# Groups of 128 rows in a streamed adjacency product: 21 blocks of 384 columns in place of 16 of 504

## What is computed

```python
# x: [8192, 64], adj: [8192, 8192], u: [8192, 64], all float32
keep = (u >= 0.1)
x_drop = x * keep / 0.9
y = x + adj @ x_drop
out = (y - mean(y)) / sqrt(var(y) + 1e-5)      # over the 64 columns of each row
```

## Time and profile before

| | |
|---|---|
| three runs, median | 643.01 us (642.99 to 643.07) |
| the profiled execution, its own time | 643.25 us |
| its span, first to last instruction | 641.5 us |
| TensorE busy with matmuls | 514.2 us, 80% |
| VectorE, ScalarE, GpSimd busy | 8%, 2%, 3% |
| moved by DMA | 274.80 MB, 428 GB/s over the span |
| TensorE's granted clock, mean | 0.93 of full |

### The profile page before, as it was taken

How to read it: one execution, slowest core, us unless ns; L and a number is a source line. 1 busy time by engine, 2 the same in 40 slices (tenths; PEclk the granted TensorE clock), 3 DMA queues, 4 the chain that set the end, 5 groups by cost and what they waited for, 6 DMA issues and landing times.

```text
span 641.5 us, 5637 instructions
## 1 busy us (share of the span) xinstructions
PE 514.2 (80%) x2308; PEld 175.9 (27%) x2308; DVE 48.6 (8%) x230; ACT 10.8 (2%) x18; POOL 18.0 (3%) x27
## 2 busy tenths in 40 slices
PE   0397888778988797797788779788797788689796
PEld 0132223222222232232232223222232232223225
DVE  2100101010010100101010010100001010000102
ACT  0000000000000000000000000000000000000000
POOL 0000000000000000000000000000000000000000
PEclk9998888998979798898989989798898989989999
DMA  9999999999999999999999999999999999999998
GB/s 374 423 448 436 429 432 440 416 440 425 430 436 450 412 449 440 429 426 443 413 440 429 430 432 454 426 432 443 423 430 439 420 437 447 428 416 428 434 422 335
DMA packets 9962, 274.80 MB, mean 428 GB/s; under 512 B 1388, under 2 KB 1642, under 8 KB 2666
## 3 DMA queue, kind: packets, MB, share of 16 engines
q1 hardware_dynamic: 9660, 274.60, 99.5%
q10 hardware_dynamic: 300, 0.16, 0.1%
HBM read 272.66 MB, written 2.10 MB: 428 GB/s over the span
## 4 chain that ended last, share of the span: by engine, by line
DMA 70%; PE 27%; issue 1%; SPq 0%; DVE 0%; POOL 0%; POOLq 0%; ACT 0%; DVEq 0%
DMA raw<-adj_dram 70%; PE acc L173 26%; SPq L132 0%; PE turned L193 0%; POOL rstd L268 0%; DVE stats L238 0%; POOLq L47 0%; ACT sums L211 0%; DVE rows L234 0%; SPq L137 0%; SPq L135 0%; SPq L136 0%; DVE moments L243 0%; POOLq L273 0%; DVE final_normed L261 0%
## 5 line engine op out<-in xcount | busy, mean ns | idle before, releaser
L173 PE MATMUL acc<-raw,dropped 128*64 128x504 f32 x2048 | 488.5, 637 | 93.3 <-POOLq L273 89.3
L173 PEld LDWEIGHTS acc<-raw,dropped 128*64 128x64 f32 x2048 | 152.9, 147 | 417.2 <-issue 291.5
L234 DVE TENSOR_TENSOR rows<-turned,x_sb 126x256 f32<-126x256 f32 x16 | 6.8, 425 | 541.8 <-PE turned L193 541.8
L268 POOL TENSOR_TENSOR rstd<-var_eps,minus_half 126x4 f32<-126x4 f32 x16 | 16.2, 1013 | 613.4 <-DMA raw<-adj_dram 330.2
L193 PE MATMUL turned<-join,sums 128*126 128x64 f32 x128 | 17.5, 279 | 10.9 <-ACT sums L211 10.9
L193 PEld LDWEIGHTS turned<-join,sums 128*126 128x126 f32 x128 | 15.3, 189 | 24.8 <-ACT sums L211 24.8
L211 ACT COPY sums<-acc 128x504 f32<-128x504 f32 x16 | 9.3, 579 | 616.3 <-PE acc L173 616.3
L249 DVE TENSOR_SCALAR normed<-rows,moments,rstd 126x64 f32 x64 | 15.7, 310 | 29.4 <-POOL rstd L268 29.4
L183 PE MATMUL final_turned<-x_final,eye 128*128 128x64 f32 x2 | 0.7, 449 | 18.1 <-DVE dropped L229 18.1
L238 DVE BATCH_NORM_STATS2 stats<-rows 126x6 f32<-126x64 f32 x64 | 9.7, 214 | 0.5
L173 PE MATMUL final_acc<-raw,dropped 128*64 128x128 f32 x128 | 7.3, 274 | 0.0
(11 more groups left out here) (14 smaller groups left out, 2.6 us busy)
## 6 DMA issues: line engine op xcount, KB each, us to landing
raw<-adj_dram SPq DMA_DIRECT2D x30, 5544.0 KB, 26.8
raw<-adj_dram SPq DMA_DIRECT2D x14, 5040.0 KB, 29.0
raw<-adj_dram SPq DMA_DIRECT2D x2, 3024.0 KB, 21.9
raw<-adj_dram SPq DMA_DIRECT2D x2, 2520.0 KB, 27.5
raw<-adj_dram SPq DMA_DIRECT2D x2, 2016.0 KB, 23.6
raw<-adj_dram SPq DMA_DIRECT2D x2, 1512.0 KB, 26.9
dropped<-u_dram SPq DMA_DIRECT2D x1, 2048.0 KB, 7.8
x_sb<-x_dram SPq DMA_DIRECT2D x1, 2048.0 KB, 12.3
```

The costliest lines, as they stand in the source:

```text
L173: last = nc.tensor.matmul(sum_bank[t * D:(t + 1) * D, 0:width], dropped[:, t * PAIRS + q, :], raw[:, s, start:start + width], start=(q == ...
L234: nc.vector.tensor_tensor(rows[:, :, :], turned[0:ROWS, 0:GROUPS, :], x_sb[0:ROWS, bass.ds(b * GROUPS, GROUPS), :], ALU.add).then_inc(turn ...
L268: nc.gpsimd.tensor_tensor(rstd[:, :], var_eps[:, :], minus_half[0:ROWS, :], ALU.pow).then_inc(rstd_ready, 1)
```

## The change

A block takes 3 groups of 128 rows, 384 columns, and there are 21 blocks; the 64th group of 128 rows is the last group. All rows of `adj` and of the output are divided as [128 partitions, 64 groups], without a remainder, and so the last group's `x` stands in `x_sb` already and its output rows lie 64 rows apart. SyncE's loop runs one block further, with whole slots, and only the last block is loaded in parts. The stores have 128 partitions in one DMA each. `PARTS`, `SLOT_PAIRS` and `FINAL` are as they were.

```diff
-ROWS = 126
-GROUPS = 4
+ROWS = P
+GROUPS = 3
-BLOCKS = CHUNKS // GROUPS
+BLOCKS = (CHUNKS - 1) // GROUPS
...
-    out_dram = out[0:ROWS * CHUNKS, :].rearrange("(p g) d -> p (g d)", p=ROWS)
+    out_dram = out.rearrange("(p g) d -> p (g d)", p=P)
...
-            sp.dma_start(x_final[:, :], x[ROWS * CHUNKS:N, :]).then_inc(x_final_loaded, DMA)
             for s in range(SLOTS):
                 load_slot(0, s)
-            with sp.Fori(1, BLOCKS - 2) as b:
+            with sp.Fori(1, BLOCKS - 1) as b:
                 for s in range(SLOTS):
                     sp.wait_ge(multiplied, (b - 1) * SLOTS + s + 1)
                     load_slot(b, s)
-            for s in range(SLOTS - 1):
-                sp.wait_ge(multiplied, (BLOCKS - 3) * SLOTS + s + 1)
-                load_slot(BLOCKS - 2, s)
-            sp.wait_ge(multiplied, (BLOCKS - 2) * SLOTS)
-            for n, (s, q0, q1) in enumerate(PARTS):
-                if s == SLOTS - 1:
-                    load_part(BLOCKS - 2, n)
...
-            for p0, p1 in [(0, EVEN), (EVEN, ROWS)]:
-                store_blocks(sp, p0, p1, 0, BLOCKS - 1)
-            sp.wait_ge(blocks_stored, 4 * DMA)
+            store_blocks(sp, 0, BLOCKS - 1)
+            sp.wait_ge(blocks_stored, 2 * DMA)
...
-            pe.wait_ge(x_final_loaded, DMA)
...
-            nc.tensor.matmul(final_turned[:, 0:D], eye[:, :], x_final[:, :], start=True, stop=False)
+            nc.tensor.matmul(final_turned[:, 0:D], eye[:, :], x_sb[:, CHUNKS - 1, :], start=True, stop=False)
...
-            for p0, p1 in [(0, EVEN), (EVEN, ROWS)]:
-                store_blocks(act, p0, p1, BLOCKS - 1, BLOCKS)
+            store_blocks(act, BLOCKS - 1, BLOCKS)
...
-            act.dma_start(out[ROWS * CHUNKS:N, :], final_normed[:, :]).then_inc(final_stored, DMA)
+            act.dma_start(out_dram[:, (CHUNKS - 1) * D:CHUNKS * D], final_normed[:, :]).then_inc(final_stored, DMA)
...
-            for s in range(1, SLOTS - 1):
+            for s in range(1, SLOTS):
                 pass_slot(BLOCKS - 2, s)
-            for n, (s, q0, q1) in enumerate(PARTS):
-                if s == SLOTS - 1:
-                    pass_part(n, 1)
-            for n, (s, q0, q1) in enumerate(PARTS):
-                pass_part(n, 2 if s == SLOTS - 1 else 1)
+            for n in range(len(PARTS)):
+                pass_part(n)
                 if n == 1:
                     rsqrt(BLOCKS - 2)
...
-    full = adj[:split].reshape(ROWS, BLOCKS, GROUPS, P, TILES, PAIRS).transpose(1, 3, 5, 4, 2, 0)
-    final = adj[split:].reshape(P, P, TILES, PAIRS).transpose(1, 3, 2, 0)
+    groups = np.asarray(adj).reshape(P, CHUNKS, P, TILES, PAIRS)
+    full = groups[:, :CHUNKS - 1].reshape(P, BLOCKS, GROUPS, P, TILES, PAIRS).transpose(1, 3, 5, 4, 2, 0)
+    final = groups[:, CHUNKS - 1].transpose(1, 3, 2, 0)
```

More of the change, by code:

```diff
@@ L29 @@
 FINAL = [(0, 8), (8, 16), (16, 22), (22, 26), (26, 29), (29, 31), (31, 32)]
-EVEN = ROWS // DMA * DMA
 P_DROP = 0.1
@@ L57, in dropout_matmul_layernorm @@
         x_sb = sbuf("x_sb", [P, CHUNKS, D])
-        x_final = sbuf("x_final", [P, D])
         dropped = sbuf("dropped", [P, CHUNKS, D])
@@ L70, in dropout_matmul_layernorm @@
         rstd = sbuf("rstd", [ROWS, GROUPS])
-        normed = sbuf("normed", [ROWS, CHUNKS, D])
+        normed = sbuf("normed", [ROWS, BLOCKS * GROUPS, D])
         final_stats = sbuf("final_stats", [P, 6])
@@ L84, in dropout_matmul_layernorm @@
         x_loaded = semaphore("x_loaded")
-        x_final_loaded = semaphore("x_final_loaded")
         u_loaded = semaphore("u_loaded")
@@ L105, in dropout_matmul_layernorm @@
         turned_free = semaphore("turned_free")
-        rows_ready = semaphore("rows_ready")
         stats_ready = semaphore("stats_ready")
@@ L116, in dropout_matmul_layernorm, with store_blocks @@
         block = ctx.enter_context(nc.Block())
-        def store_blocks(engine, p0, p1, b0, b1):
-            engine.dma_start(out_dram[p0:p1, b0 * GROUPS * D:b1 * GROUPS * D],
-                             normed[p0:p1, b0 * GROUPS:b1 * GROUPS, :]).then_inc(blocks_stored, DMA)
+        def store_blocks(engine, b0, b1):
+            engine.dma_start(out_dram[:, b0 * GROUPS * D:b1 * GROUPS * D],
+                             normed[:, b0 * GROUPS:b1 * GROUPS, :]).then_inc(blocks_stored, DMA)
         @block.sync
@@ L273, in pass_slot, with pass_part @@
                 pool.sem_inc(landed, IN_SLOT[s])
-            def pass_part(n, loads):
-                pool.wait_ge(part_loaded[n], loads * DMA)
+            def pass_part(n):
+                pool.wait_ge(part_loaded[n], DMA)
                 pool.sem_inc(landed, 1)
@@ L316 @@
     from concourse.bass_utils import run_bass_kernel_spmd
-    adj = np.asarray(adj)
-    split = ROWS * CHUNKS
-    full = adj[:split].reshape(ROWS, BLOCKS, GROUPS, P, TILES, PAIRS).transpose(1, 3, 5, 4, 2, 0)
-    final = adj[split:].reshape(P, P, TILES, PAIRS).transpose(1, 3, 2, 0)
+    groups = np.asarray(adj).reshape(P, CHUNKS, P, TILES, PAIRS)
+    full = groups[:, :CHUNKS - 1].reshape(P, BLOCKS, GROUPS, P, TILES, PAIRS).transpose(1, 3, 5, 4, 2, 0)
+    final = groups[:, CHUNKS - 1].transpose(1, 3, 2, 0)
     arrays = {
```

## The result

The changed kernel takes 644.47 us (median of 12 runs, 644.03 to 644.70) against 643.00 us for the kernel before (12 runs, 642.63 to 643.26). The ratio is 1.0022, 95% interval 1.0015 to 1.0030: slower by 0.22%, 1.47 us. The forecast was 643.6 us, with a range of 642.3 to 645.0. The range holds the time and the sign of the sum is right, but 0.59 us were forecast and 1.47 measured.

What follows compares the result with a forecast made beforehand. The loads were taken as the bound, in the middle and at the end. Twelve more loads (+0.73 us) and `x_final`'s load (-0.14) sum to +0.59 us, giving 643.6 us (+0.09%), range 642.3 to 645.0.

Steps and rivals of the forecast that it cites:

- Twelve more loads: Loads of `adj_dram` go from 56 to 68, at 0.061 us each: +0.73 us (0.62 to 2.2).
- likeliest case: The forecast itself, 643.6 us, with its own range of 643.4 to 643.9 us; chance 0.61.
- second fetch: Rival: another instruction fetch among the loads, from ScalarE's longer written-out code; 644.8 us, slower by 0.28%; chance 0.06.
- dearer rows: Rival: rows of the pieces cost more, 0.18 us a load, 645.1 us; point of decision 0.12 us; chance 0.08.
- signs of being wrong: Block at 29.15 us or more, 1.2 us loss at TensorE's third start missing or doubled, end chain changed over 0.5 us.
- Within 0.2%: Outcome of no difference a measurement can tell (0.2% is 1.3 us); chance 0.72, against slower 0.22 and faster 0.06.
- `x_final`'s load: Its 32 KB load leaves the queue ahead of all of `adj`: -0.14 us, bounds 0 and -0.46.
- The stores at nothing: Bulk and last-block stores as one DMA each, and last store's scattered rows, priced 0; last store's bounds -0.3 to +0.7 us.
- The fetch of instructions stays: Instruction packet still costs 1.16 us at TensorE's third start; rival that it moves out: 642.4 us, chance 0.11.
- The pitch: Rival: `adj` rows 96 KB apart instead of 126 KB slow the loop's reads, up to 686 us; chance 0.04.
- The reads get faster: Rival: every row now starts at a multiple of 512 B; with fetch gone and shorter end, some 641.5 us; chance 0.06.
- The scattered last store: Rival: last store's 256 B rows, now 16 KB apart, take over 0.7 us longer: 644.4 us; chance 0.03.

## Why the prediction was right, and where it was not

**The loads bound the kernel before and after, and TensorE, VectorE, GpSimd and ScalarE's added work is hidden.** Right. The five more copies, turnings and powers cost nothing; with the layout of `raw` put back, the block takes 29.093 us, where 29.09 was worked out from the loads alone.

**Twelve more loads, +0.73 us at 0.061 us each.** The mechanism was right, and so was the place; the size of this term is the step that went wrong. The price was that of slots 44352 B apart, and the change itself moved the slots. At 9.7 ns a row a whole load costs 8 x 9.7 = 78 ns, and that holds for all of them, not for the twelve: 60 x 0.078 = 4.7 us for the whole loads, where the prediction has 60 x 0.061 = 3.7. So the term was about +1.7 us instead of +0.73, and with -0.14 for `x_final` it gives the 1.6 to 1.7 us by which the last landing moved. The prediction goes through the change's edits of queues and instructions and nowhere asks how the slots of `raw` will lie: the line that declares `raw` is the same before and after.

**Why the range still held.** In part by luck. The loads cost 1.0 us more than the sum has, and the end came out 0.5 us shorter, which hid half of that. What was left lies outside the likeliest case's own 643.4 to 643.9 us; it lies inside the full range because that was drawn up to 645.0 for a second fetch and for dearer rows. By the prediction's signs of being wrong it is at the edge twice: the block's 29.145 us against 29.15, and the end's 0.5 us against 0.5. "Within 0.2%", which had 0.72, can't be told from "slower": the ratio is 1.0022, with 1.0015 to 1.0030.

**A price of each load.** It is one of each row. At 8 rows for a DMA engine in every load the two are the same, so nothing in the sum hung on it.

**`x_final`'s load, -0.14 us.** Nothing measures it alone. It is in the balance of the last landing, which closes within 0.1 us.

**The stores at nothing.** The bounds for the last store, -0.3 to +0.7 us, were missed: it became 0.4 us quicker. The prediction called the cover thin but priced only what could be lost. With the layout put back the kernel ties the one before (643.27 against 643.09 us on the same chip, +0.18), and the terms agree: 0.73 - 0.14 - 0.4 = +0.2 us.

**The fetch of instructions stays.** Right. GpSimd's pass-on of the second and the third slot's landing, each read in a stretch of 1 us (the last two numbers are first and last start):

```profile
L257 POOLq EVENT_SEMAPHORE  x1: 17/17/17, 33.4 to 33.4; - x1
```

```profile
L257 POOLq EVENT_SEMAPHORE  x1: 17/17/17, 43.9 to 43.9; - x1
```

The third comes 10.5 us after the second for 3840 KB, which at 425 KB/us and 9.7 ns a row are 9.1 us; some 1.2 to 1.4 us are lost, as in the earlier trace rows. The queues from 41 to 43 us show a packet of the instruction queue beside it, as in the earlier trace rows:

```profile
q1 hardware_dynamic: 43, 0.91, 107.8%
q8 instruction: 1, 0.02, 3.3%
```

No kernel here was built without the fetch, so that it causes the loss is argued from the coincidence in two traces and not shown.

**The rivals.** The dearer rows won in part: a load costs 0.078 us, not 0.18, and not for the reason given (short rows), but since all loads pay it, it moved the sum as far as 0.14 us on each of the twelve would, beyond the rival's point of decision of 0.12. The pitch, at two values and in both kernels, and the starts of rows in memory cost and give nothing. "The reads get faster" had noticed that every row now starts at a multiple of 512 B and took it for a gain: starts in memory gave nothing (29.144 us), and the rows became dearer, 9.7 ns for 7.7. The scattered last store did not take longer: 2.1 us for 2.5. A second fetch did not come in: the page again has two packets of the instruction queue, one between 20 and 60 us and one after 600.

## What to carry to other kernels

When a stream of loads bounds a kernel, work out the rate of its bytes and the price of a row from landings, and count rows; that gave the block's time to 0.003 us here in the one kernel that kept the buffers' layout. A change of tile shape also moves every later tensor and the distance between buffers, and this alone cost 1.2 us of 643: try the old layout before giving up a shape. And see that a whole load waits behind the one under way: with three slots it did and the stream stayed full, with two it did not and 1.5 us a block were lost. So cut loads, not slots.

## What the runs showed of the hardware

- Each row of a load costs a DMA engine some time beside its bytes: 9.1 ns where rows were added (29.145 to 29.364 us for 24 more), and 7.5 to 9.8 ns in the balance of seven kernels with the bytes taken at 435 GB/s.
- How a load's buffers lie in the partition matters to that price: 29.145 us a block with three slots 33792 B apart, 29.093 us with 44352 B. The rows of two of the three slots became about 4 ns cheaper and those of the third did not, and the extra time is there while one load alone is written and while TensorE is idle. What makes it is open.
- Reads of rows 96 KB, 96 KB + 64 B, 126 KB and 128 KB apart in memory go at the same rate, to 0.003 us in a block.
- The last store's 32 KB landed 2.5 us after issue in the kernel before, 2.1 us in the changed one, 2.2 us there with its rows in one piece, and 2.3 us with the block stores cut in two.
